# Joining the packed softmax sums on VectorE and scaling the packed outputs on GpSimd, in a two-layer attention kernel

## The reference, cut to what matters

```python
# layer 0: attention on the context, router, three experts, gate, residual
nx = layer_norm(x); weights = softmax(nx @ Wq @ (ctx @ Wk).T / 16)
combined = concat([nx, weights @ (ctx @ Wv), anchor])
x = x + sigmoid(gate(combined)) * (sum_e probs_e * expert_e(combined) @ out_w + out_b)
# layer 1: cross-attention with 16 heads of 16
q = (ada_ln(x) @ Wq + bq); k, v = split(ada_ln(ctx) @ Wkv + bkv)
attn = softmax(q @ k.T / 4)             # per head, over 154 keys
out = attn @ v                          # 16 heads of 16 columns
x = x + out @ Wp + bp
```

## Time and profile before

| what | value |
|---|---|
| median of 3 runs | 437.07 us (436.45 to 438.8) |
| the profiled execution, its own time | 438.55 us |
| the profiled execution, span of its instructions | 436.8 us |
| TensorE busy | 417.7 us (96%) |
| VectorE, ACT, GpSimd busy | 283.2, 220.0, 190.3 us (65%, 50%, 44%) |
| TensorE's granted clock, mean | 0.992 of full speed |

### The profile page before, as it was taken

The page is one execution under the profiler, slowest core; times in us unless marked ns, Lnnn a source line. Parts: engine busy times, 40 slices in busy tenths (PEclk is TensorE's granted clock), DMA queues, the critical chain, the costliest instruction groups (busy, mean ns, idle before and its releaser), DMA issues.

```text
span 436.8 us, 9535 instructions
## 1 busy us (share of the span) xinstructions
PE 417.7 (96%) x3581; PEld 379.9 (87%) x3581; DVE 283.2 (65%) x726; ACT 220.0 (50%) x487; POOL 190.3 (44%) x196
## 2 busy tenths in 40 slices
PE   7989999999999999999999999989999899979995
PEld 7578999989998899989998799879988898868874
DVE  2685566673766585748773877377557765781777
ACT  3778634245347633863367236723672366316271
POOL 6445473253543475326533663366335732441030
PEclk9899999999999999999999999999999999998999
DMA  9787001541200221124000400030003021300301
GB/s 296 239 290 281 26 2 42 159 91 30 45 4 2 57 65 29 26 56 138 2 5 13 109 2 5 13 86 2 5 19 81 0 49 32 81 5 26 72 2 50
DMA packets 16981, 27.67 MB, mean 63 GB/s; under 512 B 3816, under 2 KB 9256, under 8 KB 16808
## 3 DMA queue, kind: packets, MB, share of 16 engines
q1 hardware_dynamic: 16808, 27.06, 21.4%
q10 hardware_dynamic: 128, 0.01, 0.0%
HBM read 15.80 MB, written 2.10 MB: 41 GB/s over the span
## 4 chain that ended last, share of the span: by engine, by line
PE 81%; DVE 6%; POOL 5%; ACT 3%; issue 2%; SPq 0%; DMA 0%; POOLq 0%; ACTq 0%
PE hidden_banks L1729 8%; PE hidden_banks L1731 8%; PE hidden_banks L1730 8%; PE score_banks L1736 6%; PE token_bank L1729 6%; PE token_bank L1730 5%; PE token_bank L1731 5%; PE score_banks L2101 5%; PE value_bank L2124 3%; PE score_banks L2071 3%; PE value_bank L2127 3%; PE hidden_banks L1954 3%; PE value_bank L1736 3%; PE head_bank L1736 2%; PE score_banks L1810 1%
## 5 line engine op out<-in xcount | busy, mean ns | idle before, releaser
L1658 POOL TENSOR_TENSOR hidden_low<-hidden,hidden_high 128x512 fp32r<-128x512 f32 x56 | 72.6, 1297 | 133.0 <-ACT hidden_high L1084 133.0
L1485 DVE TENSOR_REDUCE head_maxima<-score_banks 128x2 f32<-128x308 f32 x128 | 54.0, 471 | 17.1 <-PE score_banks L2071 15.1
L1729 PE MATMUL hidden_banks<-normed_high,hidden_w_high 128*128 128x256 f32 x224 | 64.2, 287 | 0.9 <-issue 0.9
L1730 PE MATMUL hidden_banks<-normed_high,hidden_w_low 128*128 128x256 f32 x224 | 62.5, 279 | 0.0
L1731 PE MATMUL hidden_banks<-normed_low,hidden_w_high 128*128 128x256 f32 x224 | 62.4, 279 | 0.0
L1146 ACT ACTIVATE exp_ring<-score_banks 128x512 f32<-128x512 f32 x96 | 52.6, 600 | 19.2 <-PE score_banks L2101 18.3
L1076 ACT ACTIVATE hidden<-hidden_banks 128x512 f32<-128x512 f32 x56 | 33.3, 595 | 49.3 <-PE hidden_banks L1954 47.7
L1084 ACT CAST hidden_high<-hidden 128x512 fp32r<-128x512 f32 x56 | 34.8, 621 | 45.0 <-DVE hidden L1402 42.4
L1729 PE MATMUL token_bank<-expert_out_high,hidden_high 128*128 128x256 f32 x192 | 55.9, 291 | 1.5 <-POOL hidden_low L1658 1.4
L1730 PE MATMUL token_bank<-expert_out_high,hidden_low 128*128 128x256 f32 x192 | 53.5, 279 | 0.0
L1731 PE MATMUL token_bank<-expert_out_low,hidden_high 128*128 128x256 f32 x192 | 53.5, 279 | 0.0
(11 more groups left out here) (301 smaller groups left out, 1092.2 us busy)
## 6 DMA issues: line engine op xcount, KB each, us to landing
unit_weights<-units SPq DMA_DIRECT2D x7, 768.0 KB, 5.8
query_stack<-queries_high SPq DMA_DIRECT2D x56, 64.0 KB, 2.0
tokens<-x SPq DMA_DIRECT2D x8, 256.0 KB, 3.5
query_stack<-queries_low SPq DMA_DIRECT2D x28, 64.0 KB, 2.0
w_slice<-units SPq DMA_DIRECT2D x7, 256.0 KB, 2.9
out<-tokens SPq DMA_DIRECT2D x7, 256.0 KB, 2.4
w_T<-folds SPq DMA_DIRECT2D x6, 256.0 KB, 5.9
pair_keys<-keys_high SPq DMA_DIRECT2D x16, 77.0 KB
```

The lines of the kernel that those rows point to most:

```text
L1485: v.tensor_reduce(MX[:, s, first:first + step + 1:step], S[:, ring_of[key][0], 0:2 * CTX].rearrange("p (j n) -> p j n", j=2), AX.X, ALU.ma ...
L1658: nc.gpsimd.tensor_tensor(SL[:, ring(t, u), :], TB[:, ring(t, u), :], raw(SH[:, ring(t, u), :]), ALU.subtract).then_inc(gpsimd_h, 1)
L1729: mm(out_, lh, rh, start=start, stop=False, skip_group_check=skip)
L1730: mm(out_, ll, rh, start=False, stop=False, skip_group_check=skip)
```

## The change

GpSimd keeps only the first add of the sums (L1709). VectorE masks and joins the halves in tiles 0 to 6 with the two operations that it has in tile 7, in front of the reciprocal. In tiles 0 to 5 the product of the packed outputs with the spread inverse sums goes from VectorE to GpSimd, as a step mul of its own at slot 40.6; the last shuffle signals it. ACT's cast then waits for GpSimd, and stands at 38.34 + 3.3 instead of + 1.6. In tiles 6 and 7 VectorE keeps the product and signals a semaphore of its own. The bias step moves from slot 26.2 to 21.2 (tile 7 keeps its 21).

```diff
-    "out": (38.34, 56.69), "outl": (43.37, 97.85), "bias": 26.2, ...
+    "out": (38.34, 56.69), "outl": (43.37, 97.85), "bias": 21.2, "mul": 40.6, ...
-        "out": 1.6, ...                              # DELAY, scalar
+        "out": 3.3, ...
+        if t < NEXT:
+            place(at + plan(t, "mul"), ("mul", t))
@@ ScalarE, outs
-                act.wait_ge(vector_out, upto(vector_out, key, "o"))
+                if t < NEXT:
+                    act.wait_ge(gpsimd_mul, upto(gpsimd_mul, ("mul", t), "o"))
+                else:
+                    act.wait_ge(vector_scaled, t - NEXT + h + 1)
@@ VectorE, sums
                 if t == LAST:
                     dve.wait_ge(scalar_raw, upto(scalar_raw, ("raw", t, h), "v"))
+                    even, odd = RAWL[:, 2 * h, :], RAWL[:, 2 * h + 1, :]
                 else:
                     dve.wait_ge(gpsimd_sum, upto(gpsimd_sum, ("sum", t), "s"))
+                    even, odd = (out_tiles(t)[0][:, o, :] for o in range(2))
+                v.tensor_scalar(total[:, :], even, other_rows, None, ALU.mult).then_inc(vector_results, results.one())
+                dve.wait_ge(vector_results, results.n)
+                v.scalar_tensor_tensor(out=total[:, :], in0=odd, scalar=own_rows, in1=total[:, :],
+                                       op0=ALU.mult, op1=ALU.add).then_inc(vector_results, results.one())
+                dve.wait_ge(vector_results, results.n)
                 v.reciprocal(total[:, :], total[:, :]).then_inc(vector_sums, 1)
@@ VectorE, outs
-                dve.wait_ge(vector_results, results.n)
-                v.tensor_tensor(packed[:, g, :], packed[:, g, :], spread[:, g, :], ALU.mult).then_inc(vector_out, 1)
+                if t >= NEXT:
+                    dve.wait_ge(vector_out, upto(vector_out, key, "s"))
+                    v.tensor_tensor(packed[:, g, :], packed[:, g, :], spread[:, g, :], ALU.mult).then_inc(vector_scaled, 1)
@@ GpSimd, new
+            def scale(key):
+                t = key[1]
+                pool.wait_ge(vector_out, upto(vector_out, ("out", t, 0), "s"))
+                pool.wait_ge(vector_dup, upto(vector_dup, ("dup", t, 0), "d"))
+                spread, _, _, packed = out_tiles(t)
+                nc.gpsimd.tensor_tensor(packed[:, :, :], packed[:, :, :], spread[:, :, :], ALU.mult).then_inc(gpsimd_mul, 1)
@@ GpSimd, sums
-                nc.gpsimd.tensor_tensor(both[:, :, :], RAW[:, 0:2, :], RAW[:, 2:4, :], ALU.add).then_inc(gpsimd_part, 1)
-                pool.wait_ge(gpsimd_part, 3 * t + 1)
-                nc.gpsimd.tensor_scalar(both[:, 0, :], both[:, 0, :], other_rows, None, ALU.mult).then_inc(gpsimd_part, 1)
-                nc.gpsimd.tensor_scalar(both[:, 1, :], both[:, 1, :], own_rows, None, ALU.mult).then_inc(gpsimd_part, 1)
-                pool.wait_ge(gpsimd_part, 3 * t + 3)
-                nc.gpsimd.tensor_tensor(SUM[:, :], both[:, 0, :], both[:, 1, :], ALU.add).then_inc(gpsimd_sum, 1)
+                nc.gpsimd.tensor_tensor(both[:, :, :], RAW[:, 0:2, :], RAW[:, 2:4, :], ALU.add).then_inc(gpsimd_sum, 1)
```

More of the change, by code:

```diff
@@ L222 @@
         "sums": ["r"],
-        "out": ["o"],
+        "out": ["s"],
         "outl": ["l"],
@@ L242 @@
         "bias": ["x"],
+        "mul": ["o"],
         "sum": ["s"],
@@ L254 @@
         "logit": 1.7, "z": 0.81, "h": 0.3, "gate": 0.4, "qx": 0.4, "query": 0.1, "row": -0.4, "score": 0.2,
-        "out": 1.6, "xhat_last": -0.7, "qx_last": 0.2, "query_last": 0.2, "row_last": 0.5, "score_last": 0,
+        "out": 3.3, "xhat_last": -0.7, "qx_last": 0.2, "query_last": 0.2, "row_last": 0.5, "score_last": 0,
         "raw_last": 0.1, "out_last": 1.54,
@@ L285 @@
     "value": (33.88, 34.18, 35.92, 35.93), "raw": (35.5, 36.9), "sum": 36.4, "sums": (38.1, 47.7),
-    "out": (38.34, 56.69), "outl": (43.37, 97.85), "bias": 26.2, "proj": 43.6, "last": (16, 59.3), "reload": 45.3, "init": 5.2,
+    "out": (38.34, 56.69), "outl": (43.37, 97.85), "bias": 21.2, "mul": 40.6, "proj": 43.6, "last": (16, 59.3), "reload": 45.3, "init": 5.2,
 }
@@ L696, in build @@
         proj_b_loaded = sem("proj_b_loaded")
+        vector_scaled = sem("vector_scaled")
         stored = sem("stored")
@@ L1531, in outs @@
                     v.stream_shuffle(spread[:, i, :], sums_of(t, h)[:, :], [sum_row(2 * i)] * DH + [sum_row(2 * i + 1)] * DH).then_inc(
-                        vector_results, results.one())
-                dve.wait_ge(vector_results, results.n)
-                v.tensor_tensor(packed[:, g, :], packed[:, g, :], spread[:, g, :], ALU.mult).then_inc(vector_out, 1)
+                        vector_out if i == g.stop - 1 else vector_results, 1 if i == g.stop - 1 else results.one())
+                if t >= NEXT:
+                    dve.wait_ge(vector_out, upto(vector_out, key, "s"))
+                    v.tensor_tensor(packed[:, g, :], packed[:, g, :], spread[:, g, :], ALU.mult).then_inc(vector_scaled, 1)
             def outs_low(key):
@@ L1704, in sums @@
                 if t:
-                    pool.wait_ge(vector_out, upto(vector_out, ("out", t - 1, 0), "o"))
+                    pool.wait_ge(vector_out, upto(vector_out, ("out", t - 1, 0), "s"))
+                    pool.wait_ge(gpsimd_mul, upto(gpsimd_mul, ("mul", t - 1), "o"))
                 if t == NEXT:
@@ L1708, in sums @@
                 both = out_tiles(t)[0]
-                nc.gpsimd.tensor_tensor(both[:, :, :], RAW[:, 0:2, :], RAW[:, 2:4, :], ALU.add).then_inc(gpsimd_part, 1)
-                pool.wait_ge(gpsimd_part, 3 * t + 1)
-                nc.gpsimd.tensor_scalar(both[:, 0, :], both[:, 0, :], other_rows, None, ALU.mult).then_inc(gpsimd_part, 1)
-                nc.gpsimd.tensor_scalar(both[:, 1, :], both[:, 1, :], own_rows, None, ALU.mult).then_inc(gpsimd_part, 1)
-                pool.wait_ge(gpsimd_part, 3 * t + 3)
-                nc.gpsimd.tensor_tensor(SUM[:, :], both[:, 0, :], both[:, 1, :], ALU.add).then_inc(gpsimd_sum, 1)
+                nc.gpsimd.tensor_tensor(both[:, :, :], RAW[:, 0:2, :], RAW[:, 2:4, :], ALU.add).then_inc(gpsimd_sum, 1)
             parts = {"setup2": setup_values, "gsplit": gate_split, "unit": unit, "split": split, "keyn": keyn, "ln": ln, "norm": norm, "prob": prob,
-                     "low": low, "h": hidden, "qn": qn, "zero": zeros, "sel": select, "bias": projection_bias, "sum": sums}
+                     "low": low, "h": hidden, "qn": qn, "zero": zeros, "sel": select, "bias": projection_bias, "mul": scale, "sum": sums}
             for key in order("gpsimd"):
```

7 lines of the change are left out of this document (1 added, 6 removed).

## The result

The changed kernel took 434.5 us in the median (433.69 to 436.64) where the kernel before, run beside it, took 438.27 (436.23 to 439.7). The ratio is 0.9923 (95% interval 0.9907 to 0.9938): 3.4 us less, between 2.7 and 4.1 (the two medians by themselves lie 3.8 apart). The forecast was 3.4 us less, and its 433.7 us against a median of 437.07 is a ratio of 0.992. The profiled execution took 434.88 us with a span of 433.1; the one before had 438.55 and 436.8.

A forecast was written before the change was run, and what follows sets the result against it. TensorE, busy 96% of the span, was taken as the bound, except where it waits and in a tail chain of GpSimd then VectorE. Gains of 2.0 + 0.1 + 0.4 + 0.9 = 3.4 us gave 433.7 us, range 432.3 to 434.9.

The forecast's parts named there:

- TensorE's stalls in tiles 0, 2 and 3: TensorE's waits for GpSimd's hidden_low and VectorE's reduce at the sums: 0.65 us gained per tile, 2.0 us together.
- The lock: Rival: VectorE and GpSimd exclude each other at the sums, leaving 0.2 us per tile; 435.6 us in all, chance 0.18.
- the L1186 row: Tile 1's two-column VectorE operation, 0.90 us instead of 0.17, ending with hidden_low; cited for the lock, about 0.7 us lost.
- The row that the prediction set against a full block: VectorE's L1520 ran 0.85 us from 416.86 while GpSimd's L1711 ran from 416.64 to 417.63; cited against a full block.
- The product on GpSimd: Tiles 0 to 5: relieves VectorE of 0.69 us per tile; in tiles 0 to 4 only keeps it ahead.
- The bias step: Bias add moved 5 slots ahead into GpSimd's idle time: cost nothing; without that cover 1.29 us for the following hidden_low.
- Tile 4's stretch: Tile 4, where no rstd runs and the product's delay is nearly all VectorE's: 0.1 us gained (0 to 0.4).
- ACT's cast: Moved behind GpSimd's product, in ACT's idle time before the next hidden_high: hidden, 0.8 us to spare.
- the slower rival: GpSimd's late product holds ACT's queue; each microsecond beyond 0.8 us passes to TensorE six times; 439.7 at 1.8 us late, chance 0.05.
- Tile 5: VectorE's reduces come 0.9 us early, shortening TensorE's losses before the last maxima: 0.4 us gained, bounds 0 and 0.9.
- The tail: Tile 6's sums to the last products: reciprocal 0.9 us sooner, all in the chain; at most 1.0 us can pass.
- The sum: Whole kernel: 2.0 + 0.1 + 0.4 + 0.9 = 3.4 us less, 433.7 us against a median of 437.07.

The follow-up runs named there:

- experiment 10: The full change with VectorE's two joining operations made twice in tiles 0 to 5: 447.58 us, ratio 1.0221 to the kernel before.
- experiment 11: The full change with only the first joining operation (the mask, a tensor_scalar) made twice in tiles 0 to 5: 439.94 us, ratio 1.004 to the kernel before.
- experiment 12: The full change with two more two-input VectorE operations behind the join in tiles 0 to 5: 448.3 us, ratio 1.0225 to the kernel before.
- experiment 2: The full change without VectorE's joining in tiles 0 to 6: GpSimd keeps all four sums operations and gets the product; 438.52 us, ratio 1.0009 to the kernel before.
- experiment 8: The full change with GpSimd's product made twice in tiles 0 to 5, so ACT's cast waits longer: 434.77 us, ratio 0.9926 to the kernel before.
- experiment 3: The kernel before, with the joining on VectorE in tile 6 alone: 436.83 us, ratio 0.997 to the kernel before.
- experiment 5: The full change, but tile 6's bias add waits until VectorE's expert_sum operations are done: 433.45 us, ratio 0.9903 to the kernel before.
- experiment 9: The full change with tile 6's bias add held until the expert_sum operations end, plus 24 filler matmuls in TensorE's waits: 432.9 us, ratio 0.9889 to the kernel before.
- experiment 6: The full change, but the bias step stays at its old slot 26.2 in all tiles: 434.47 us, ratio 0.9929 to the kernel before.

## Why the prediction was right

- **TensorE's stalls in tiles 0, 2 and 3 (predicted 0.65 each, 2.0 together).** What TensorE lost ahead of the stalled product, over the issue time of the work before it, was 1.06, 1.11 and 0.96 us and is 0.36, 0.33 and 0.31: 0.70, 0.78 and 0.65, together 2.1. The split between GpSimd (0.7) and VectorE (0.3) holds: the 0.3 that is left is VectorE's, as the stretches of experiments 10 to 12 grow by what VectorE comes late there (in full in tiles 3 and 4, where no fall of the clock is added), and experiment 2 shows that without GpSimd's part nothing moves. The reciprocal came 0.51 us nearer to the add in tile 3 of this pair, and 0.12 nearer against experiment 2, where the query stack was in time as in after (4.30 behind the add); 0.2 was forecast.
- **The lock (0.7 us per tile as its price, 0.18 as its chance).** As a mechanism it is real, and dearer than the L1186 row made it: experiments 10 to 12 measured 0.9 to 1.1 us for each operation held. The change escapes it because the second joining operation starts before hidden_low, by 0.43 us in tile 3 and by 0.10 in tile 1. That the slots fell so was luck, as the prediction doesn't give this order as its reason. I had argued from GpSimd's gaps between its add and 290 and had never compared the two starts that decide; my rows had both (about 290.2 and 290.6). The rule of the Trainium skill, "SBUF — State Buffer", section "Who interferes with whom", that VectorE with two SBUF inputs and GpSimd reading SBUF exclude each other, and that the one which issues first goes first, is what experiments 11 and 12 show; it also names the tensor_scalar of experiment 10. The hold beside probs is no weaker, only shorter. A held operation ends after its holder by its own length less about 0.2 us: 0.16 of 0.34 and 0.28 of 0.49 in experiments 10 and 11, and 0.54 of 0.75 for L1528 behind the first probs. The row that the prediction set against a full block stood beside GpSimd's tensor_scalar, and there the measurement does differ from the rule. In tile 3 of before GpSimd's L1711 starts first, yet VectorE's L1518 takes 0.47 us, as in after, and L1711 1.13 us, where tile 0's L1712, of the same form, takes 0.92:

```profile
287.58 1.13 POOL L1711 TENSOR_SCALAR sums_spread<-sums_spread,constants 128x256 f32<-128x256 f32 x1
...
288.00 0.47 DVE L1518 TENSOR_SCALAR outs_packed<-outs_and_sums,constants 128x512 f32<-128x512 f32 x1
```

- **The product on GpSimd (cost and gain nothing in tiles 0 to 4).** Right for tiles 0 to 4: 1.28 us there, with no stall of TensorE behind it. What the product's move brings, it brings in tile 5.
- **The bias step ("Cost nothing").** The step that failed. I had looked for cover on GpSimd's queue alone, and it was idle; the cost came on VectorE, 0.60 us in one tile. Tile 4's stretch, 0.40 longer instead of 0.1 shorter, is this less a gain of 0.20.
- **ACT's cast (0.8 us to spare).** Hidden as forecast. Experiment 8 shows that the price of the slower rival, six times what goes beyond 0.8 us, was wrong: a product 1.3 us later passed nothing to TensorE in tiles 0 to 4 and about 0.4 us in tile 5, and there by GpSimd's own hidden_low.
- **Tile 5 (0.4).** 40.42 with before's body and no fall of the clock (experiment 3), 39.99 after: 0.43. Experiment 2 gets 0.41 of it by the product's move alone. The join alone gets 0.30 (41.57 against before's 41.87, both with a fall of the clock), so the two overlap and don't add.
- **The tail (0.9, at most 1.0).** 0.96 in the profile. In medians, −0.3% in experiment 3, 1.3 us with an interval from 0.4 to 2.3.
- **The sum.** 2.1 + 0.2 + 0.4 + 0.96 − 0.6 = 3.1 us, where 3.4 was forecast and 3.4 (2.7 to 4.1) measured. Errors of some tenths went opposite ways (0.2 too little for the stalls and tile 4, 0.6 too much for the bias step), so that the measured 3.4 is the forecast to the tenth is luck; the mechanism is not. What made the profiled pair differ by 3.7 in span holds 0.9 of transfer waits, and a fall of the clock and a prologue that came to −0.5. Why the stack's transfer is late in some executions and not in others stays open.

## What to carry to other kernels

Where operations of two engines exclude each other, don't ask whether they overlap but which of two named instructions starts first and by how much; write that margin down, because a delay of 0.38 us in each tile turned a gain of 3.4 us into a loss. An operation moved into another engine's idle time needs cover on both sides: idle there, and nothing on the neighbour that it locks out. Where a part of a change measures as nothing, look whether two terms cancel in it. And test how tight a path is by making an operation on it twice: it showed within one run that VectorE's path from the sums to the reduces is TensorE's, one for one in tiles 0, 2, 3 and 4, which the busy share of 66% hides.

## What the runs showed of the hardware that was not expected

- A VectorE operation of 128x256 held by GpSimd's 128x512 subtraction ends 0.16 us (tensor_scalar, alone 0.34) to 0.3 us (two-input, alone 0.49) after it. It was held when its record began 0.04 us earlier (experiment 11, four tiles, 41 to 45 ns) and not when it began 0.05 us earlier (tile 4, 48 ns); then the subtraction took 1.59 us instead of 1.29.
- The granted clock fell to its lower level in some executions and not in others: in before's stretch 5 to 6 (six matmuls took 1.63 us instead of 0.98) but not in after's or experiment 3's, behind the same wait of 2.19 us; in the prologues of before and after; nowhere in experiments 5, 9 and 11. Waits of 1.86 to 1.91 us were followed by it in two tiles of four in experiment 10, waits of 1.93 to 2.03 us in the same two of four in experiment 12, waits of 1.5 us in none of three in experiment 11, but shorter ones of 0.75 and 0.49 us once in experiment 6. Where a kernel without the fall stands beside it, a fall cost 1.0 to 1.7 us, up to half of what the whole change is worth, so a single profiled pair could not have measured it.
